# Attention: another table of probability buffers, and the maxima of the next unit begun at step 8

## The reference

```python
q = heads(x @ Wq)                                   # 16 heads of 32
k_s, v_s = heads(x @ Wkv_short); k_l, v_l = heads(x @ Wkv_long)
bias = -abs(pos[None, :] - pos[:, None]) * (1 - decay_factor)
out_short = softmax(q @ k_s.T / sqrt(32) + bias) @ v_s     # 2048 x 2048 scores
out_long  = softmax(q @ k_l.T / sqrt(32)) @ v_l
out = alpha * out_short + (1 - alpha) * out_long
```

## Time and profile before

| | us |
|---|---|
| median of three runs | 4771.02 (4766.81 to 4774.06) |
| the profiled execution | 4764.1 |
| its span, first to last instruction | 4762.1 |
| PE busy in the span | 4467.5 (94%) |
| DVE, POOL, ACT busy | 3788.4 (80%), 3088.7 (65%), 2982.2 (63%) |

### The profile page before, as it was taken

One profiled execution on the slowest core, in us unless ns is written; L12 is line 12 of the kernel. 1 busy time (PEld: TensorE's weight loads), 2 busy tenths in 40 slices (PEclk: granted clock), 3 DMA queues, 4 the chain that ended last, 5 costly groups with the idle time before them and its releaser, 6 DMA issues. The chain is left out here.

```text
span 4762.1 us, 157195 instructions
## 1 busy us (share of the span) xinstructions
PE 4467.5 (94%) x61452; PEld 2434.6 (51%) x61452; DVE 3788.4 (80%) x4400; ACT 2982.2 (63%) x5297; POOL 3088.7 (65%) x1236
## 2 busy tenths in 40 slices
PE   8999799999999999999999999999995899999998
PEld 3444244444444555444444444444442677777776
DVE  7657788888888888888888888888781688888887
ACT  3222377777777777777777777777774455555553
POOL 0000389898989898988989888889885333333332
PEclk9999699999999999999999999999997899999999
DMA  5444376767666667667767666676754000000000
GB/s 168 138 127 123 86 150 139 156 143 153 144 146 142 151 146 156 137 145 146 151 144 151 143 144 144 144 153 144 151 107 117 21 28 21 28 28 21 28 23 12
DMA packets 242106, 547.41 MB, mean 115 GB/s; under 512 B 71471, under 2 KB 145327, under 8 KB 200561
## 3 DMA queue, kind: packets, MB, share of 16 engines
q0 software_dynamic: 45792, 333.47, 35.4%
q1 hardware_dynamic: 195563, 203.94, 15.0%
q10 hardware_dynamic: 38, 0.08, 0.0%
HBM read 140.34 MB, written 62.16 MB: 43 GB/s over the span
## 5 line engine op out<-in xcount | busy, mean ns | idle before, releaser
L983 DVE TENSOR_REDUCE rowmax_parts<-scores_qk 128x1 f32<-128x1024 f32 x2048 | 2414.8, 1218 | 514.4 <-PE scores_qk L1068 509.7
L961 ACT ACTIVATE probs_T<-scores_kq 128x512 f32<-128x512 f32 x3840 | 2069.3, 602 | 535.0 <-PE scores_kq L1068 379.0
L868 POOL TENSOR_TENSOR probs_added<-probs_added,probs_T 128x2048 f32<-128x2048 f32 x446 | 2093.9, 4695 | 48.0 <-POOL probs_added L868 38.1
L1068 PE MATMUL scores_kq<-q_operand,k_operand 103*32 103x512 f16 (+3 forms) x13312 | 1239.5, 372 | 126.5 <-DMA q_operand_above<-negmax_T 68.8
L1068 PE MATMUL scores_qk<-k_operand,q_operand 96*32 96x512 f16 (+4 forms) x13312 | 1050.7, 373 | 27.9 <-DMA v_operand<-v_dram 14.2
L1150 PE MATMUL outputs_T<-probs_T,v_operand 128*32 128x512 f32 x7680 | 1029.1, 598 | 6.4 <-issue 5.6
L1068 PEld LDWEIGHTS scores_kq<-q_operand,k_operand 103*32 103x32 f16 x13312 | 396.5, 96 | 692.5 <-ACT probs_T L961 275.8
L1068 PEld LDWEIGHTS scores_qk<-k_operand,q_operand 102*32 102x32 f16 (+1 forms) x13312 | 385.9, 98 | 512.6 <-issue 229.8
L1758 PE MATMUL f_gate_up<-w_gate_up,xq_T 128*128 128x256 f16 (+1 forms) x4608 | 494.2, 266 | 7.6 <-DVE hidden L1649 6.5
L868 POOL TENSOR_TENSOR probs_added<-probs_T 128x2048 f32<-128x2048 f32 x64 | 292.0, 4563 | 292.4 <-DVE probs_T L1012 239.3
L1758 PEld LDWEIGHTS f_gate_up<-w_gate_up,xq_T 128*128 128x128 f16 x4608 | 421.0, 98 | 77.0 <-issue 24.3
(11 more groups left out here) (173 smaller groups left out, 4570.0 us busy)
## 6 DMA issues: line engine op xcount, KB each, us to landing
probs_poured<-probs_T POOLq DMA_DIRECT2D x318, 1024.0 KB, 8.7
qk_parts_dram<-qk_parts SPq DMA_DIRECT2D x96, 256.0 KB, 2.8
q_operand<-qk_parts_dram SPq DMA_DIRECT2D x192, 128.0 KB, 3.4
k_operand<-qk_parts_dram SPq DMA_DIRECT2D x192, 128.0 KB, 7.4
v_dram<-v_heads SPq DMA_DIRECT2D x16, 1024.0 KB, 6.4
v_operand<-v_dram SPq DMA_DIRECT2D x64, 256.0 KB, 6.7
sums_inverse<-sums_inverse_dram SPq DMA_DIRECT2D x64, 256.0 KB
q_operand_above<-qk_parts_dram SPq DMA_DIRECT2D x96, 128.0 KB, 4.1
```

The lines of the kernel that those rows point to most:

```text
L868: nc.gpsimd.tensor_tensor(total, first, block_of(w, b), ALU.add).then_inc(added.sem, 1)
L961: nc.scalar.activation(block_of(w, kb)[:, qt * BANK:(qt + 1) * BANK], pb[:, ring_of(c) % BANKS, :], ACT.Exp).then_inc(expd.sem, 1)
L983: nc.vector.reduce_max(rowmax[:, w % 2, g // 2, g % 2:g % 2 + 1], half, AX.X).then_inc(maxed.sem, 1)
L1068: mm = nc.tensor.matmul(out[j:j + HD, :], lhsT[:, j:j + HD], rhs, start=start, stop=stop, skip_group_check=True)
```

## The change

Four edits in `attend`:

- `ASTEPS` goes from 10 to 8: steps 0 to 7 do the last eight steps' worth of the next unit's maxima, steps 8 to 15 the first eight of the unit after it. Ahead of unit 0, eight steps' worth of unit 1 are done instead of six.
- `TURN_MAX` goes from 10 to 8: the transposition stands in step 8. The inverse stays in step 10.
- SP's queue in a unit becomes `pack_sums` twice, `place_max`, `store_inverse`, `spread_inverse`.
- Buffers go by the table `SLOT`: blocks 1 to 14 in seven buffers, block b in (b - 1) % 7, and block 15 alone in the eighth. `block_free` waits for the block before in the table's order.

Which block a block now follows in its buffer (the unit before is "last"):

| block | before | after |
|---|---|---|
| 1 to 6 | last 9 to 14 | last 8 to 13 |
| 7 | last 15 | last 14 |
| 8 | last 8 | own 1 |
| 9 to 14 | own 1 to 6 | own 2 to 7 |
| 15 | own 7 | last 15 |

```diff
--- before.py
+++ after.py
@@ -590,13 +590,13 @@
 NPOS = 6
 MROW = PARTS3 + NPOS
 
-ASTEPS = 10
+ASTEPS = 8
 
 SQUARE = 32
 COMPACT = L // P
 INVERT = 10
 JOIN = 4
-TURN_MAX = 10
+TURN_MAX = 8
 
 
 VISIT = 1
@@ -611,6 +611,8 @@
 POURS = len(BY_DMA)
 POOL_ORDER = (1, 4, 5, 6, 7, 8, 9, 10, 11, 12, 13, 14, 15)
 WEIGH_BEHIND = 14
+ALONE = 15
+SLOT = {b: k % (PBUF - 1) for k, b in enumerate(b for b in range(1, KB) if b != ALONE)} | {ALONE: PBUF - 1}
 DIRECT = range(12, KB)
 
 
@@ -719,7 +721,7 @@
 
         def block_of(w, kb):
 
-            return poured_sum[:, w % 2, :] if kb == 0 else probs[:, kb % PBUF, :]
+            return poured_sum[:, w % 2, :] if kb == 0 else probs[:, SLOT[kb], :]
 
         def load_positions(eng, w):
 
@@ -810,10 +812,10 @@
                     if back:
                         for j in range(2):
                             pack_sums(*back, j)
-                        store_inverse(*back)
                     if after(w, n, last):
                         place_max(*after(w, n, last))
                     if back:
+                        store_inverse(*back)
                         spread_inverse(*back)
                     if w == 1 and not first:
                         store(1, n - 1)
@@ -919,7 +921,8 @@
                 if kb == 0:
                     act.wait_ge(counted[1].sem, counted[1].at(n, w - 1))
                     return
-                u, b = (w, kb - PBUF) if kb > PBUF else (w - 1, kb + PBUF) if kb < PBUF else (w - 1, kb)
+                same = [b for b in range(1, KB) if SLOT[b] == SLOT[kb]]
+                u, b = (w, same[0]) if kb > same[0] else (w - 1, same[-1])
                 act.wait_ge(summed.sem, summed.at(n, u * KB + b + 1))
                 if b == JOINED[0]:
                     act.wait_ge(joined.sem, joined.at(n, u + 1))
```

## The result

The changed kernel takes 4819.48 us, the median of five runs (4799.01 to 4834.5); the kernel before took 4772.54 on the same chip, the median of four runs beside a fifth of 22184.14 that is left out. The ratio is 1.0100, with an interval of 1.0083 to 1.0116: slower by 0.8 to 1.2%. The forecast was 4824 us. The profiled execution took 4819.84 us with a span of 4818.0, against 4764.1 before, so 55.7 us are to be found in it.

The account below looks back on a forecast made before the run. PE does most of a 96.09 us pair, with POOL's additions and pours a second chain behind it. Loop 95.47 plus clock 2.25 is 97.72 a pair, +49, with the prologue +53 us: 4824 us, range 4747 to 4855.

Parts of the forecast that it names:

- Maxima two steps earlier: At long units' ends: this edit alone would take away PE's 64.3 us of waits and the low clock behind them.
- Prologue, +4: Ahead of unit 0, eight more chunks of maxima cost 4 us (bounds 0 and 4.7).
- Block 8 behind pour 1, met at the count in step 7: In a long unit block 8 waits for pour 1's landing; PE waits 4.1 us at step 7's count.
- The loop: Short unit's first addition through pour 1's landing and the count to the next first addition: at least 95.47 us a pair.
- The low clock, 2.25 us a pair: Behind the wait at step 7's count PE runs at 1.2 GHz, losing 2.25 us a pair (bounds 0 and 3.00).
- The long unit takes all of it: The short unit has none of the new wait; the long unit's is 4 to 5 us.
- the loop without it (4756): Rival: same wait, but the clock stays up or both units share it; pair 95.47 us, 4756 us; chance 0.22.
- 4661: Rival: pour 1 lands after 8.2 us, the loop is 90.8 us and does not bind, 4661 us; chance 0.08.
- 4854: Rival: SP's eight transfers take 5 us longer, half the old wait stays, 1 us a pair, 4854 us; chance 0.05.

Follow-up runs that it names:

- number 5: The changed kernel with block 15 left out of the sum of probabilities, so without pour 15: 4628.69 us, ratio 0.9691.
- the kernel with both edits: The changed kernel with the next unit's pour 1 issued ahead of pour 15 and the poured sum's count in step 8, not 7: 4728.43 us, ratio 0.9910.
- the later inversion: The kernel with both edits, with the merge and inversion of the sums in step 12 of VectorE's order, not 10: 4735.23 us, ratio 0.9932.
- number 11: The changed kernel with nine more products of the next unit's maxima ahead of the count in step 7 of every unit: 4802.83 us, ratio 1.0058.

## Why the prediction held, point by point

- *Maxima two steps earlier.* Right: the wait of 64.3 us is gone in the changed kernel, and the moved store and spread cost nothing that shows. Alone this edit gains 34 us; the prediction said that it would take away the 64.3 us and the low clock behind them, and about half of that is taken back at blocks 4 and 7. So this sentence of the prediction was too large for the edit alone.
- *Prologue, +4.* Right: 3.9 us.
- *Block 8 behind pour 1, met at the count in step 7.* Right, and shown by three runs: the table alone has the wait, exchanging blocks 8 and 9 gives back 68 us, and without pour 15 it goes. First addition to landing stayed at 56.0 us (the median of the short units; 55.2 in the long ones).
- *The loop.* Its terms hold to 0.2 us in units 46 and 47, but for the stall there. Over the 18 pairs of units 4 to 59 that have the wait in the long unit they are less exact: on the mean 56.2 us to the landing (55.95 forecast), 0.8 to PE, 25.3 from the count to the unit's end (26.27 with the clock) and 16.3 from the next start to the first addition (14.74). The last was put too small by 1.6 us: 1.0 of that is stalls of PE without a named releaser, which the sum had at nothing, and 0.5 the low clock behind three of them. In the whole stage such stalls grew from 29.7 to 44.8 us.
- *The low clock, 2.25 us a pair.* Right in kind, too large in size. Of the 28 waits of over 1 us ahead of the count in units 4 to 59, which make 3.4 us a pair, 22 have the lower level of 1.2 GHz granted within 1.5 us of the count's start; behind six (of 1.62, 1.74, 2.10, 2.17, 2.36 and 2.87 us) the clock stays up there. In the 12 us behind these counts the lower level is granted for 86.1 us in all; half of that is lost, 1.5 us a pair. The Trainium skill, "TensorE: Matmul & The Clock Gate", section "HAM oscillation — how this bites in real kernels", has each recurring wait start the next tile at half clock; here most do, and the trace agrees better than that of before did, where by the same count 11 of 31 did (the prediction has 12; one more begins 5.9 us behind its wait). The stage in this kernel, then in the kernel before (granted clock 0.98 and 0.99):

```profile
560.00:3560.00 3000.00, 2837.70 (x48972) 1421.08 (x48964) 2462.95 (x2262) 2215.28 (x4096) 2603.09 (x883) 0.98 0.68 142
```

```profile
560.00:3560.00 3000.00, 2866.92 (x49796) 1405.66 (x49788) 2510.01 (x2302) 2238.78 (x4168) 2648.61 (x899) 0.99 0.68 145
```

- *"The long unit takes all of it".* Wrong in 11 of 33 waits. The same argument holds for both kinds (each closes its own loop of the same pieces), so a stall can hand the wait from one to the other; what handed it over at unit 24 and back behind unit 42 I can't show. It is one wait a pair either way, and the sum hardly moves: a pair takes 97.47 us from unit 4 to 24 and 97.26 from 24 to 44.
- *The rivals.* The clock fell, so the loop without it (4756) fell; pour 1 still lands 12.9 us behind its issue (4661 fell); nobody waits for the transfers (4854 fell).
- *Pour 6 behind pour 1's landing* (34.1 us on POOL) was missing from the working. It seems to cost little here, since the short unit's chain keeps its length, which no run tests by itself; and it is what the experiments with other tables ran into.

The distance to the forecast, 4.5 us, is within the spread of the runs. The direction and the chain behind it were foreseen; that the pair came within 0.2 us (97.90 for 97.72) is in part luck, since the clock's term was some 0.7 us too large and the stalls, which the sum did not have, made up for much of it.

## What to carry to other kernels

Before a buffer is given to another user, look up when its last reader lets go in time, not in the order of the blocks: a landing behind another transfer in the same queue comes later than its length says (12.9 us in the median against 7.6 here). When a wait is removed, follow the freed engine to the next thing that it meets, and add that chain up over a whole period; here it was 0.6 us shorter than the old period, and so the ceiling of every gain that this change could bring. A wait that is moved can be longer than those removed, and then it also costs clock.

## What the runs showed of the hardware

Of two accumulating transfers of 1 MB issued some 0.6 us apart in one queue, the first lands after 7.0 to 9.6 us over all runs (medians 7.3 to 8.3), much as pour 1 alone does in number 5 (7.0 to 9.2, median 7.6), and the second after 11.3 to 13.8 (medians 12.8 to 12.9), whichever blocks they carry. The Trainium skill, "DMA: Bandwidth & Descriptors", section "Anatomy of one DMA — SWDGE (gpsimd) path", fits one transfer issued from GpSimd by 2.0 us and its bytes over 436 GB/s; for 1 MB that is an estimate of 4.4 us. The pours here, which add while they move from buffer to buffer on the chip, take 6.9 us or more, so the measurement decides.

PE's stalls without a named releaser often come back 28 units apart, which is one turn of the unrolled loop (in the kernel with both edits, step 10 of units 16 and 44 and of 22 and 50 takes 5.0 to 5.7 us in place of 2.7). They grow from 25.9 us where pour 15 is left out to 67.2 us with both edits and 81.7 us behind the later inversion (lines of the scores alone). The traces say more than the view of waits does: one DMA queue, q8, is of the kind "instruction" and moves 498 pieces of 16 KB in every run but number 11, where PE has more products to do and the queue moves 516. Of the 247 such stalls of over 1 us in the stage, over all thirteen runs, 242 end 1.2 to 1.8 us behind the end of one of these transfers; of PE's 348 other waits of that length 63 do. One stall of unit 44 in the kernel with both edits, and the queue from 2674.4 to 2675.6 us, where its one transfer ends at 2675.48:

```profile
2676.92 0.35 PE L1075 MATMUL scores_qk<-k_operand,q_operand 102*32 102x384 f16 x4 [2.06 <-issue]
```

```profile
q8 instruction: 1, 0.02, 4.9%
```

So these stalls are most likely waits for PE's own code. That is read from the times and the counts; no run was made to test it, and why the stalls grow from kernel to kernel stays open.
